# The last image of a vision layer: terms of seven states scaled token-major by ScalarE and transposed into PSUM by TensorE, the image before it finished in 24 half steps

## The chip, the cores and the metric

The kernel runs on one core of a Trainium2 chip. The metric is the device time of one execution in microseconds. A core has five engines with instruction queues of their own that work in program order: TensorE (PE; its weight loads are shown as PEld), VectorE (DVE), ScalarE (ACT), GpSimd (POOL) and SyncE (SP), which here only issues transfers. They meet in semaphores: an instruction raises one when it is done, another engine's queue waits for its value.

## The reference

Four images of 1024 tokens with 64 features pass one layer. It has a retention part, a selective scan and a routed feed-forward part, with a layer norm behind each of the last two:

```python
# retention
q, k, v = x @ Wq + bq, x @ Wk + bk, x @ Wv + bv
h = prelu(((gamma * (q @ k.T)) @ v) @ Wo + bo)
# selective scan, 128 channels, 16 states each
x_main, x_gate = split(h @ W_in + b_in)
xc = silu(x_main @ W_conv + b_conv)
B, C = split(xc @ W_bc + b_bc)                  # 16 numbers of each per token
dt = softplus(xc @ W_dt + b_dt)
for t in range(1024):
    s = exp(dt[t][:, None] * A) * s + dt[t][:, None] * B[t][None, :] * xc[t][:, None]
    y[t] = (s * C[t][None, :]).sum(-1)
h = layernorm(h + (y * silu(x_gate)) @ W_out + b_out)
# feed-forward: 64 groups of 64 tokens, each with its own expert
f = relu(h @ Wi.T + bi)
for l in range(2): f = relu(f @ shared[l] + f @ expert[l, route] + biases + f)
h = layernorm(h + f @ Wo.T + bo)
```

## The kernel before

The 128 channels of the scan lie on the partitions, the tokens along the free dimension. For each state a *job* computes `h[t] = decay[t] * h[t-1] + u[t] * B[t]` with one scan instruction of VectorE (L1336), where `decay = exp(delta * neg_a[state])` and `u = delta * xc`. Then `hc = h * C` is made ("weighed") by GpSimd (`weigh`, L1207), and TensorE adds hc, transposed, to the bank `acc_y` (`states_out`, L663). B and C are rows in DRAM (`bc_dram`), which SyncE loads broadcast over all partitions into `b_row` and `c_row` (three buffers each).

A job of the first three images has 1024 tokens. In the last image (`SPLIT`, `ALONE`) there are 32 jobs of 512 tokens: 16 states of the first half of the tokens, then the same 16 of the second. The last h of a job of the first half is kept in `carry` and starts the job of the same state in the second; ScalarE copies it (`save_carry`, L957).

The term u*B is made in one of two ways. For a job of `VECTOR_JOBS` ScalarE copies u into a PSUM bank (`fill_slot`, L947; the name `slot` is shown as `decay` in the trace), VectorE multiplies it there by b_row (`drive`, L1308), and ScalarE puts the decay into `decay_own` (`own_decay`, L920). For the others GpSimd multiplies u by b_row into `ub` (`drive`, L1196) and ScalarE puts the decay into the slot (L920). The slot has two banks, taken in turn by the jobs, so a bank can be filled for job t when the scan of job t-2 is done.

The order of work is written out by hand. All engines run the same loop, `for p in PHASES: for n in range(STEPS)`; phase p scans image p, while the head of image p+1 and the tail of image p-1 go on beside it. In the last phase each step n has two half steps, 2n and 2n+1, one for each job. In a half step s of that phase ScalarE fills the slot for job s+2, does its part of the third image's tail (`last_part`) and of the first half of the last image's own tail (`half_tail(0)`), and then makes `decay_own` for job s+3. VectorE scans job s, then its parts of the tails. GpSimd weighs job s-2, then drives job s+2. TensorE issues a matmul that keeps its clock up (`keep_warm`), `states_out` of job s-4, then its parts of both tails.

The third image's tail is a chain of 19 parts m over TensorE, ScalarE and VectorE that share the one bank `tail`: y transposed (m=2), the output product (3, 4), the norm (4 to 6), the feed-forward input (6, 7), two expert layers (8 to 13), output (13, 14), norm (15, 16), rows (17, 18). Part m is done in half step `2 + 8 * m // 5` (L295). The tables `HALF_PE`, `HALF_ACT` and `HALF_DVE` give the half steps 20 to 31 to the parts of `half_tail(0)`: y at 20, norm 22 and 23, expert layers from 25 and 27, second norm 29 and 30. After the last scan `end_of_program` does the same for the second half of the tokens.

Before the last phase, in phase 2, the head of the last image makes its bc (n=10), delta (n=12) and u (n=13).

Of the kernel before, what the change touches and what calls it, by code (L numbers as in the profile page):

```python
# [23 lines left out]
P = 128  # L24
# [22 lines left out]
for _b in range(IMAGES):  # L47
    for _first in (0, HALF) if _b in SPLIT else (0,):
        for _s in range(STATES):
# [6 lines left out]
VECTOR_JOBS = [q for q, job in enumerate(JOBS)  # L56
               if job.state in ((0, 4, 8, 10, 14) if job.image not in SPLIT else range(0, STATES, 2))]
GPSIMD_JOBS = [q for q in range(len(JOBS)) if q not in VECTOR_JOBS]
# [37 lines left out]
LAST_STEPS = 19  # L96
RELUS = (USE_L1, USE_L1 + 1, USE_L2, USE_L2 + 1)
# [33 lines left out]
def vit_layer(nc, xT, gammaT, packed, routed_w, route, out):  # L131
    with ExitStack() as ctx:
# [56 lines left out]

        late_w = gam[:, 4:8, :].rearrange("p a (g l h) -> p (a g) l h", l=LAYERS, h=HID)  # L190
# [43 lines left out]
        carry_saved = sem("carry_saved")  # L234
        hc_own = sem("last_hc_by_vector_ready")
# [53 lines left out]
        def last_steps(p, n, i):  # L289
# [44 lines left out]
        def gpsimd_made(q):  # L334

            return JOBS[q].at - vector_made(q)
# [9 lines left out]
        def ub_made(q):  # L346

            return (ub_own, vector_made(q) + JOBS[q].halves) if on_vector(q) else (ub_ready, gpsimd_made(q) + JOBS[q].halves)

# [64 lines left out]
        def _(sp):  # L414
# [26 lines left out]
            def load_b(k):  # L441
# [79 lines left out]
        def _(pe):  # L521
# [145 lines left out]

            def begin_tail(b, use):
# [159 lines left out]
            for p in range(-1, IMAGES):  # L828
                for n in range(STEPS):
# [7 lines left out]
                    for i, (start, end) in enumerate(parts(p, n)):  # L837
# [65 lines left out]
        def _(act):  # L903
# [20 lines left out]
            def own_decay(q):  # L924

                made, halves = vector_made(q), JOBS[q].halves
                if made >= 2:

                    act.wait_ge(scan_done, end_of(job_with(vector_made, VECTOR_JOBS, made + halves - 3)))
# [22 lines left out]
            def save_carry(q):  # L952

                job = JOBS[q]
                act.wait_ge(scan_done, end_of(q))
                at = ring(job.at, 1).stop - 1
                nc.scalar.activation(carry[:, job.state:job.state + 1], h[:, at:at + 1], ACT.Copy).then_inc(carry_saved, 1)  # L957
# [69 lines left out]
            def last_part(b, n):  # L1027
# [4 lines left out]
                if b == ALONE - 1 and DVE_TAIL.get(n) in RELUS:  # L1032
# [528 lines left out]
```

## Time and profile before

| what | value |
|---|---|
| median of 3 runs | 344.54 us (343.37 to 346.07) |
| the profiled execution | 343.26 us |
| its span in the profile | 340.9 us |
| mean granted TensorE clock | 0.915 |
| busy share PE, DVE, ACT, POOL | 83, 77, 56, 76 % |

The span runs from the first to the last instruction of the profiled execution. A busy share is a mean over stages with different limits, so the stage of the last image has to be read by itself.

### The profile page before, as it was taken

The page shows a single profiled execution, that of the slowest core. Times are in us where ns is not written, and L with a number is a line of the kernel's source. Part 1 is how long each engine was busy: PE and PEld are TensorE (multiplying, and loading weights), DVE is VectorE, ACT ScalarE, POOL GpSimd, SP SyncE. Part 2 cuts the span into 40 slices and gives each one's busy share as a digit, 9 for nine tenths or more (in the row PEclk, how much of TensorE's full clock was granted, in tenths as well). Part 3 has the DMA queues.
Part 4 walks back from the last instruction along what each step waited for, and adds up shares of the span by engine and source line. Part 5 has one row for each costly group of instructions (what it writes and reads, how often), then busy time and mean ns, then how long its engine had stood idle before and what let it go on. Part 6 is the DMA issues. An engine that isn't in the chain of part 4 may idle for free.

```text
span 340.9 us, 4748 instructions
## 1 busy us (share of the span) xinstructions
PE 284.1 (83%) x1462; PEld 164.4 (48%) x1462; DVE 262.5 (77%) x287; ACT 190.5 (56%) x298; POOL 259.4 (76%) x136
## 2 busy tenths in 40 slices
PE   8898839875677789989896799996975989977896
PEld 5423412333336233355662344565854668755664
DVE  2565678998778999998899799988979899575420
ACT  3004831336896342589855516799277768655422
POOL 1028057999899999998998969989999999993200
PEclk9999957999589799999799799996598999978999
DMA  7970496676779997866799967668999999980200
GB/s 236 409 294 0 147 317 218 211 280 215 249 278 308 343 358 260 285 256 232 306 279 329 344 217 273 216 244 287 296 326 330 329 376 362 301 278 25 48 0 15
DMA packets 47128, 85.88 MB, mean 252 GB/s; under 512 B 7936, under 2 KB 24832, under 8 KB 46848
## 3 DMA queue, kind: packets, MB, share of 16 engines
q1 hardware_dynamic: 46704, 84.43, 73.7%
q10 hardware_dynamic: 400, 1.17, 1.1%
q8 instruction: 11, 0.18, 0.2%
q14 instruction: 13, 0.11, 0.1%
HBM read 75.62 MB, written 1.57 MB: 226 GB/s over the span
## 4 chain that ended last, share of the span: by engine, by line
PE 28%; DVE 15%; ACT 12%; issue 4%; POOL 2%; DVEq 0%; ACTq 0%; POOLq 0%
DVE h L1336 10%; PE acc_y L663 5%; PE tail L722 4%; ACT decay L920 2%; PE acc_r L616 2%; PE work L605 2%; DVE decay L1308 2%; POOL ub L1196 2%; PE tail L677 1%; PE tail L707 1%; PE work L539 1%; PE decay L539 1%; ACT decay_own L920 1%; PE work L754 1%; PE tail L698 1%
## 5 line engine op out<-in xcount | busy, mean ns | idle before, releaser
L1207 POOL TENSOR_TENSOR hc<-h,c_row 128x1024 f32<-128x1024 f32 (+1 forms) x79 | 154.6, 1966 | 24.3 <-DVE h L1336 20.9
L1196 POOL TENSOR_TENSOR ub<-u,b_row 128x1024 f32<-128x1024 f32 (+1 forms) x49 | 98.3, 2006 | 11.5 <-DVE u L1382 11.1
L920 ACT ACTIVATE decay<-delta,neg_a 128x512 f32<-128x512 f32 (+1 forms) x64 | 51.4, 813 | 64.0 <-DVE h L1336 63.5
L663 PEld LDWEIGHTS acc_y<-pack,hc 128*128 128x128 f32 x512 | 62.7, 150 | 43.0 <-issue 23.3
L663 PE MATMUL acc_y<-pack,hc 128*128 128x128 f32 x512 | 76.0, 291 | 6.7 <-ACT y_t L1030 3.6
L1336 DVE TENSOR_TENSOR_SCAN h<-decay,ub 128x512 f32<-128x512 f32 (+1 forms) x41 | 65.9, 1608 | 11.5 <-ACT decay L920 5.7
L605 PE MATMUL work<-q,kT 64*128 64x512 f32 x112 | 36.4, 729 | 16.3 <-DVE mixed L1362 11.9
L1362 DVE TENSOR_TENSOR mixed<-gam,work 128x512 f32<-128x512 f32 x56 | 35.6, 676 | 8.2 <-PE work L605 7.5
L947 ACT ACTIVATE decay<-u 128x512 f32<-128x512 f32 (+1 forms) x42 | 26.4, 639 | 21.8 <-DVE h L1336 21.5
L616 PE MATMUL acc_r<-mixed,v_sb 128*64 128x512 f32 x128 | 36.4, 648 | 1.1 <-DVE mixed L1362 1.0
L1336 DVE TENSOR_TENSOR_SCAN h<-decay_own,decay 128x512 f32<-128x512 f32 (+1 forms) x23 | 34.5, 1499 | 1.1
L1308 DVE TENSOR_TENSOR decay<-decay,b_row 128x512 f32<-128x512 f32 (+1 forms) x40 | 30.6, 764 | 6.0 <-ACT decay L947 4.3
L920 ACT ACTIVATE decay_own<-delta,neg_a 128x512 f32<-128x512 f32 (+1 forms) x31 | 28.5, 919 | 1.4 <-DVE delta L1375 1.4
L722 PEld LDWEIGHTS tail<-f,group_w 128*128 128x128 f32 x192 | 26.3, 213 | 0.4
L722 PE MATMUL tail<-f,group_w 128*128 128x64 f32 x192 | 25.6, 293 | 0.0
L605 PEld LDWEIGHTS work<-q,kT 64*128 64x128 f32 x112 | 9.5, 207 | 32.9 <-DVE mixed L1362 22.5
L1336 DVE TENSOR_TENSOR_SCAN h<-decay,h,ub 128x512 f32<-128x512 f32 x18 | 23.1, 1283 | 2.5
L1181 POOL TENSOR_TENSOR expert_w<-expert_w 128x2048 f32<-128x2048 f32 x2 | 9.0, 4541 | 15.2 <-DMA expert_w<-routed_w 15.2
L616 PEld LDWEIGHTS acc_r<-mixed,v_sb 128*64 128x64 f32 x128 | 6.7, 143 | 28.0 <-issue 19.7
L1336 DVE TENSOR_TENSOR_SCAN h<-decay_own,h,decay 128x512 f32<-128x512 f32 x9 | 11.5, 1280 | 0.3
L539 PE MATMUL work<-gam 128*128 128x256 f32 x36 | 11.7, 413 | 0.0
L986 ACT ACTIVATE hT<-acc_r,pack 128x512 f32<-128x512 f32 x4 | 2.7, 674 | 15.8 <-PE acc_r L616 15.8
(208 smaller groups left out, 356.6 us busy)
## 6 DMA issues: line engine op xcount, KB each, us to landing
b_row<-bc_dram SPq DMA_DIRECT2D x64, 512.0 KB, 5.4
c_row<-bc_dram SPq DMA_DIRECT2D x64, 512.0 KB, 5.5
group_w<-expert_w SPq DMA_DIRECT2D x48, 128.0 KB, 4.7
gam<-gammaT SPq DMA_DIRECT2D x8, 512.0 KB, 10.6
expert_w<-routed_w SPq DMA_DIRECT2D x1, 2048.0 KB, 18.3
gam<-expert_w SPq DMA_DIRECT2D x16, 128.0 KB, 5.3
x_in<-xT SPq DMA_DIRECT2D x4, 256.0 KB, 8.6
pack<-packed ACTq DMA_DIRECT2D x1, 788.0 KB, 6.6
```

What stands on the lines that cost most here:

```text
L539: nc.tensor.matmul(bank[:, 0:2 * INNER], gam[:, 0, 0:P], gam[:, 0, 0:2 * INNER], start=True, stop=True)
L605: nc.tensor.matmul(pair[:, i * HALF:(i + 1) * HALF], kT[D * i:D * i + D, j * P:(j + 1) * P], q2[D * i:D * i + D, :], start=True, stop=True ...
L616: mm = nc.tensor.matmul(acc_r[D * i:D * i + D, :], v_sb[:, j, :], mixed[:, j % 2, i * HALF:(i + 1) * HALF], start=(j == 0), stop=(j == TIL ...
L663: mm = nc.tensor.matmul(acc_y[:, to:to + P], hc[:, at:at + P], ident, start=(job.state == 0 and c % 4 == 0), stop=(job.state == STATES - 1 ...
L722: mm = nc.tensor.matmul(bank[:, (g % 8) * GROUP:(g % 8 + 1) * GROUP], group_w[:, g, layer, :], f[:, g * GROUP:(g + 1) * GROUP], start=Fals ...
L920: op = nc.scalar.activation(target, delta[:, job.image % 2, columns], ACT.Exp, scale=neg_a[:, job.state:job.state + 1])
L947: nc.scalar.activation(slot[:, two_banks(at, halves)], u[:, job.image % 2, columns], ACT.Copy)\
L1196: nc.gpsimd.tensor_tensor(ub[:, ring(made, job.halves)], u[:, job.image % 2, tokens(q)], b_row[:, ring(job.at, job.halves)], ALU.mult).the ...
L1207: nc.gpsimd.tensor_tensor(hc[:, here], h[:, here], c_row[:, here], ALU.mult).then_inc(hc_ready, job.halves)
L1308: nc.vector.tensor_tensor(slot[:, here], slot[:, here], b_row[:, columns], ALU.mult).then_inc(ub_own, halves)
L1336: nc.vector.tensor_tensor_scan(h[:, ring(at, halves)], factor, term, initial, ALU.mult, ALU.add)\
L1362: nc.vector.tensor_tensor(mixed[:, j % 2, at], gam[:, j, at], pair[:, at], ALU.mult).then_inc(read, 1)
```

## The change

`PLACED_STATES` gives seven even states (2 to 14) of the last image, in both halves of its tokens, a third way. TensorE transposes u of the whole image (`transpose_u`, eight transposes) and bc (`transpose_bc`, two); ScalarE reads both out to SBUF (`read_u_t`, `read_bc_t`). With tokens on the partitions B[t] is one number per partition: ScalarE multiplies four 128x128 tiles of the transposed u by it (`scale_terms`), and TensorE transposes them into the job's slot bank (`place_terms`), where the scan reads them. Of the last image's 32 jobs 14 are placed, 6 are VectorE's own (states 0, 5, 11; 16 jobs before), and 12 are GpSimd's (16 before). Where only one of a pair of states still needs its row, half of b_row is loaded. ScalarE's `save_carry` becomes a copy by VectorE behind its scan. The four relus of the third image's expert layers go from ScalarE to VectorE. The third image's tail gets a table of half steps, `TAIL_AT`, that ends at 23 in place of 30. In half steps 24 to 31 TensorE issues a `keep_warm` matmul each, as it did only in 2 to 19.

```diff
+PLACED_STATES = {IMAGES - 1: (2, 4, 6, 8, 10, 12, 14)}
+PLACED_JOBS = [q for q, job in enumerate(JOBS) if job.state in PLACED_STATES.get(job.image, ())]
+VECTOR_JOBS = [q for q, job in enumerate(JOBS) if job.state in ((0, 4, 8, 10, 14) if job.image not in SPLIT else (0, 5, 11))]
+KEPT_JOBS = sorted(VECTOR_JOBS + PLACED_JOBS)
+GPSIMD_JOBS = [q for q in range(len(JOBS)) if q not in KEPT_JOBS]
...
+TAIL_AT = (2, 3, 4, 5, 6, 7, 9, 10, 12, 13, 14, 15, 17, 18, 19, 20, 21, 22, 23)
...
+        u_t = {0: y_t, ALONE: kT}
+        bc_t = {0: ln_x, ALONE: x_in}
+        placed_rows = {0: (f[:, :], f[:, :]), ALONE: (q2[:, :], v_sb[:, :, :].rearrange("p c d -> p (c d)"))}
...
-                steps += [(p - 1, m) for m in range(LAST_STEPS) if 2 + 8 * m // 5 == 2 * n + i]
+                steps += [(p - 1, m) for m in range(LAST_STEPS) if TAIL_AT[m] == 2 * n + i]
...
-                        sp.wait_ge(*ub_made(q))
-                sp.dma_start(into(b_row, k), rows(k, 0)).then_inc(b_loaded[k % 3], 16)
+                        if q not in PLACED_JOBS:
+                            sp.wait_ge(*ub_made(q))
+                wanted = [q for q in begun(2 * k, 2 * k + 2) if q not in PLACED_JOBS]
+                if b in SPLIT and len(wanted) == 1:
+                    job = JOBS[wanted[0]]
+                    sp.dma_start(b_row[:, ring(job.at, 1)],
+                                 bc_dram[b, job.state, tokens(wanted[0])].partition_broadcast(P)).then_inc(b_loaded[k % 3], 16)
+                elif wanted:
+                    sp.dma_start(into(b_row, k), rows(k, 0)).then_inc(b_loaded[k % 3], 16)
...
+            def transpose_u(b):
+
+                pe.wait_ge(u_ready, b + 1)
+                if b == ALONE:
+                    pe.wait_ge(work_read, FIRST_WORK_USES + WORK_USES * ALONE)
+                for i in range(2):
...
+                    for c in range(TILES // 2):
+                        at = i * HALF + c * P
+                        mm = nc.tensor.transpose(target[:, c * P:(c + 1) * P], u[:, b % 2, at:at + P], ident)
+                    mm.then_inc(u_t_full, 1)
+
+            def place_terms(q):
+
+                job = JOBS[q]
+                pe.wait_ge(term_ready, placed_made(q) + job.halves)
+                pe.wait_ge(scan_done, job.at + job.halves - 2)
+                rows_sb = placed_rows[job.image][placed_made(q) % 2]
+                for c in range(job.halves * TILES // 2):
+                    at = two_banks(job.at, job.halves).start + c * P
+                    mm = nc.tensor.transpose(slot[:, at:at + P], rows_sb[:, c * P:(c + 1) * P], ident)
+                mm.then_inc(term_placed, job.halves)
...
                         if p == ALONE and WARM_FROM <= 2 * n + i < WARM_TO:
 
+                            if 2 * n + i == WARM_FROM:
+                                pe.wait_ge(u_t_read, 2 * order_of_placed(ALONE) + 2)
                             keep_warm(work[:, HALF:T], 1)
+                        if p == ALONE and 2 * n + i >= 24:
+                            if 2 * n + i == 24:
+                                pe.wait_ge(tail_read, TAIL_SETUP + TAIL_USES * ALONE)
+                            keep_warm(tail, 1)
+                        for q in begun(start + 1, end + 1) if p == ALONE else begun(start + 2, end + 2):
+                            if q in PLACED_JOBS and (p == ALONE or JOBS[q].image == 0):
+                                place_terms(q)
                         for q in ended(start - 4, end - 4):
                             states_out(q)
...
+                    if head == ALONE and n == 11:
+                        transpose_bc(ALONE)
+                    if head == ALONE and n == 14:
+                        transpose_u(ALONE)
...
-            def save_carry(q):
...
+            def scale_terms(q):
...
+                if placed_left(q):
+                    act.wait_ge(term_placed, placed_left(q))
+                rows_sb = placed_rows[job.image][made % 2]
+                for c in range(job.halves * TILES // 2):
+                    token = job.first // P + c
+                    at = token % 2 * P + 2 * STATES * (token // 2) + job.state
+                    op = nc.scalar.activation(rows_sb[:, c * P:(c + 1) * P], u_t[job.image][:, token * P:(token + 1) * P],
+                                              ACT.Identity, scale=bc_t[job.image][:, at:at + 1])
+                op.then_inc(term_ready, job.halves)
...
-                if b == ALONE - 1 and DVE_TAIL.get(n) in RELUS:
-                    use = DVE_TAIL[n]
...
+                    if head == ALONE and n == 15:
+                        read_u_t(ALONE)
                     for i, (start, end) in enumerate(parts(p, n)):
                         for q in begun(start + 2, end + 2):
-                            fill_slot(q)
+                            if q not in PLACED_JOBS:
+                                fill_slot(q)
...
-                            if own_limit(start) <= JOBS[q].at < own_limit(end) and on_vector(q):
+                            if own_limit(start) <= JOBS[q].at < own_limit(end) and q in KEPT_JOBS:
                                 own_decay(q)
+                                if q in PLACED_JOBS:
+                                    scale_terms(q)
+                    if head == ALONE and n == 12:
+                        read_bc_t(ALONE)
...
+                if job.halves == 1 and job.first == 0:
+
+                    dve.wait_ge(scan_done, end_of(q))
+                    last = ring(job.at, 1).stop - 1
+                    nc.vector.tensor_copy(carry[:, job.state:job.state + 1], h[:, last:last + 1]).then_inc(carry_saved, 1)
...
-                if use in RELUS and b < ALONE - 1:
+                if use in RELUS:
```

## Rows read from the trace of the kernel before

**Rows 1.** The page, part 1: busy us (share of span) xinstructions.
```profile
PE 284.1 (83%) x1462; PEld 164.4 (48%) x1462; DVE 262.5 (77%) x287; ACT 190.5 (56%) x298; POOL 259.4 (76%) x136
```

**Rows 2.** Busy us by stretch: PE, PEld, DVE, ACT, POOL, clock, DMA share, GB/s.
```profile
251.00:280.00 29.00, 22.05 (x121) 16.19 (x119) 26.48 (x29) 22.49 (x50) 28.11 (x23) 0.94 1.05 342
280.00:320.60 40.60, 33.76 (x221) 26.50 (x221) 27.16 (x30) 24.75 (x49) 31.12 (x26) 0.92 0.69 222
302.50:309.00 6.50, 6.42 (x26) 5.62 (x27) 2.12 (x2) 2.02 (x4) 5.23 (x5) 0.53 0.63 208
```

**Rows 3.** GpSimd in order of time: start us, us, line, out<-in [idle before <-releaser].
```profile
258.52 2.50 POOL L1207 TENSOR_TENSOR hc<-h,c_row 128x512 f32<-128x512 f32 x2 [0.16 <-DMA c_row<-bc_dram]
...
262.63 2.50 POOL L1207 TENSOR_TENSOR hc<-h,c_row 128x512 f32<-128x512 f32 x2
265.10 1.26 POOL L1196 TENSOR_TENSOR ub<-u,b_row 128x512 f32<-128x512 f32 x1
...
313.68 2.49 POOL L1207 TENSOR_TENSOR hc<-h,c_row 128x512 f32<-128x512 f32 x2 [5.95 <-DVE h L1336]
```

**Rows 4.** VectorE in order of time, an earlier stage and the last one.
```profile
213.94 1.22 DVE L1336 TENSOR_TENSOR_SCAN h<-decay,ub 128x512 f32<-128x512 f32 x1
215.30 1.28 DVE L1336 TENSOR_TENSOR_SCAN h<-decay,h,ub 128x512 f32<-128x512 f32 x1
...
251.08 0.70 DVE L1308 TENSOR_TENSOR decay<-decay,b_row 128x512 f32<-128x512 f32 x1 [1.27 <-ACT decay L947]
...
255.70 1.22 DVE L1336 TENSOR_TENSOR_SCAN h<-decay_own,decay 128x512 f32<-128x512 f32 x1
256.84 1.20 DVE L1336 TENSOR_TENSOR_SCAN h<-decay,ub 128x512 f32<-128x512 f32 x1
...
279.95 0.67 DVE L1308 TENSOR_TENSOR decay<-decay,b_row 128x512 f32<-128x512 f32 x1
...
297.91 0.42 DVE L1426 TENSOR_TENSOR gam<-gam,work 128x256 f32<-128x256 f32 x1 [2.51 <-ACT work L1095]
...
310.68 0.69 DVE L1406 TENSOR_TENSOR ln_y<-ln_x,tail 128x512 f32<-128x512 f32 x1 [5.92 <-ACT tail L1049]
...
319.33 1.27 DVE L1336 TENSOR_TENSOR_SCAN h<-decay,carry,ub 128x512 f32<-128x512 f32 x1
```

**Rows 5.** VectorE in order of time, two small operations of the setup.
```profile
34.41 0.14 DVE L1301 COPY b_c<-tail 128x2 f32<-128x2 f32 x1
34.48 0.27 DVE L1286 CAST bias_w<-pack 96x256 bf16<-96x256 f32 x1
```

**Rows 6.** ScalarE in order of time: ahead of the stage, and in it.
```profile
248.68 0.69 ACT L1041 ACTIVATE ln_q<-tail,b_c 128x512 f32<-128x512 f32 x1 [0.68 <-PE tail L698]
...
260.52 0.59 ACT L947 ACTIVATE decay<-u 128x512 f32<-128x512 f32 x1
261.04 0.19 ACT L957 ACTIVATE carry<-h 128x1 f32<-128x1 f32 x1
261.13 0.68 ACT L920 ACTIVATE decay<-delta,neg_a 128x512 f32<-128x512 f32 x1
261.75 0.19 ACT L957 ACTIVATE carry<-h 128x1 f32<-128x1 f32 x1
...
295.28 0.47 ACT L1082 ACTIVATE gam<-acc_r,b_c 128x256 f32<-128x256 f32 x1
295.64 0.47 ACT L1086 ACTIVATE gam<-acc_r,b_c 128x256 f32<-128x256 f32 x1
```

**Rows 7.** TensorE in order of time, the last stage.
```profile
260.15 0.63 PE L663 MATMUL acc_y<-pack,hc 128*128 128x128 f32 x4 [3.58 <-ACT y_t L1030]
...
267.59 1.08 PE L698 MATMUL tail<-f,w_out_c 128*64 128x512 f32 x4
...
279.14 1.89 PE L722 MATMUL tail<-f,group_w 128*128 128x64 f32 x16
...
281.36 0.60 PE L663 MATMUL acc_y<-pack,hc 128*128 128x128 f32 x4
281.80 0.60 PE L539 MATMUL work<-gam 128*128 128x256 f32 x2
```

More of the change, by code:

```diff
@@ L348, in ub_made, with b_loads @@
             return (ub_own, vector_made(q) + JOBS[q].halves) if on_vector(q) else (ub_ready, gpsimd_made(q) + JOBS[q].halves)
+        def b_loads(k):
+            return 16 * sum(s % 3 == k % 3 and any(q not in PLACED_JOBS for q in begun(2 * s, 2 * s + 2)) for s in range(k + 1))
         def ring(at, halves):
@@ L950, in fill_slot, with read_bc_t, read_u_t @@
                         decay_exp(q, slot[:, two_banks(at, halves)], columns)
-            def save_carry(q):
[L954 to L957, printed above, removed]
+            def read_bc_t(b):
+                act.wait_ge(bc_t_full, order_of_placed(b) + 1)
+                if b == 0:
+                    act.wait_ge(s_bias, BIAS_STEPS)
+                source = acc_r if b == ALONE else tail
+                nc.scalar.activation(bc_t[b][:, 0:2 * P], source[:, 0:2 * P], ACT.Copy).then_inc(bc_t_read, 1)
+            def read_u_t(b):
+                before = 2 * order_of_placed(b)
+                for i in range(2):
+                    columns = slice(i * HALF, (i + 1) * HALF)
+                    act.wait_ge(u_t_full, before + i + 1)
+                    source = work[:, columns] if b == ALONE else tail[:, :]
+                    nc.scalar.activation(u_t[b][:, columns], source, ACT.Copy).then_inc(u_t_read, 1)
+            def scale_terms(q):
+                job, made = JOBS[q], placed_made(q)
+                if job.image == ALONE and made == placed_made(PLACED_JOBS[0]) or q == PLACED_JOBS[0] or \
+                        JOBS[PLACED_JOBS[PLACED_JOBS.index(q) - 1]].image != job.image:
+                    act.wait_ge(u_t_read, 2 * order_of_placed(job.image) + 2)
+                    act.wait_ge(bc_t_read, order_of_placed(job.image) + 1)
+                if placed_left(q):
[7 more added lines that the diff above has]
+                op.then_inc(term_ready, job.halves)
             def first_evictions():
@@ L1138, in _ @@
                             side_eviction(head, SIDE_AT[n])
-                        for q in ended(start, end):
-                            if JOBS[q].halves == 1 and JOBS[q].first == 0:
-                                save_carry(q)
                         for b, m in last_steps(p, n, i):
@@ L1216, in _ @@
                         for q in begun(start + 2, end + 2):
-                            if not on_vector(q):
+                            if q in GPSIMD_JOBS:
                                 drive(q)
@@ L1316, in scan_job @@
                     here = two_banks(at, halves)
-                    if on_vector(q):
-                        drive(q, here, ring(at, halves), vector_made(q) + done)
-                        factor, term = decay_own[:, two_banks(vector_made(q) + at - job.at, halves)], slot[:, here]
+                    if q in KEPT_JOBS:
+                        if on_vector(q):
+                            drive(q, here, ring(at, halves), vector_made(q) + done)
+                        else:
+                            dve.wait_ge(term_placed, placed_made(q) + job.halves)
+                        factor, term = decay_own[:, two_banks(kept_made(q) + at - job.at, halves)], slot[:, here]
                     else:
@@ L1325, in scan_job @@
                         dve.wait_ge(hc_ready, at + halves - 6)
-                        old = JOBS[JOB_OF[at + halves - 7]]
-                        if old.halves == 1 and old.first == 0:
-                            dve.wait_ge(carry_saved, old.state + 1)
                     initial = 0.0
```

52 lines of the change are left out of this document (39 added, 13 removed).

## The prediction, made before the changed kernel ran

> **What bounds the kernel now.** I read first the page's busy shares [rows 1]: TensorE, VectorE and GpSimd are all at 76 to 83 per cent, so the whole-span average names nobody, and the question is what ends last in the stage that the diff touches. That is the last image's scan stage: its 32 half steps (one job of 512 tokens each, which I call step 0 to step 31) run from VectorE's first multiply at 251.08 us to the end of the last scan at 320.60 us, 69.5 us. Behind it lies a fixed end of 20.3 us (the second half's feed-forward part), which the diff leaves as it is.
>
> The busy times by stretch [rows 2] and GpSimd's order of time [rows 3] show the first 56 us of it: GpSimd is busy 28.11 of 29.00 us in steps 0 to 15. Two weighings take 2.47 us and a drive 1.27, so two steps cost it 3.7 us. VectorE (26.48 of 29.00) keeps pace just behind. In steps 16 to 31 the picture is another: 40.6 us, of which VectorE works 27.2. Its order of time [rows 4] shows where the rest went: a wait of 2.51 us at 297.91 and one of 5.92 us at 310.68, both for ScalarE's logarithm step of a layer norm. The second is the third image's last norm, which stands behind the last image's own layers on TensorE. GpSimd then idles too, 5.95 us [rows 3]. So there are two things to win: GpSimd's load, and that collision.
>
> **The change, part by part.** Times are summed against the profiled execution (343.26 us: 340.9 of span and 2.4 around it). The median of the runs is 1.28 us above it, and I carry that over.
>
> *GpSimd.* 16 drives in the stage become 12. Four fewer at about 1.24 us of spacing is 5.0 us, which leaves 44 operations, 54.6 us. The b_row loads of 14 of the 16 pairs halve; GpSimd hardly waits for them now [rows 3], so this gives nothing by itself.
>
> *VectorE.* 16 multiplies become 6. Each costs 0.70 us between its start and the scan behind it (251.08 and 279.95 are such multiplies; the duration is 0.67 to 0.70): ten are 7.0 us, five of them in each half. Four relus of 512 columns come over from ScalarE; a multiply of that width lasts 0.67 to 0.70, and without a wait behind it I put one at 0.6: 2.4 us, half in each half. The 16 carry copies come over too, each with a wait for VectorE's own scan, all in steps 0 to 15. A scan with no such wait is followed after 1.14 us (255.70 to 256.84), one whose successor waits for it after 1.36 us (213.94 to 215.30) [rows 4]; a 128x2 copy keeps the engine 0.07 us (34.41 to 34.48) [rows 5]. So a carry costs at most 0.22+0.07 = 0.29 and at least 0.07; I take 0.26, nearest to the row with the wait, 4.2 us in all. Steps 0 to 15: 26.5 - 3.5 + 1.2 + 4.2 = 28.4 us of VectorE work, more than the 26.5 before. Steps 16 to 31: 27.2 - 3.5 + 1.2 = 24.9.
>
> A rule of the Trainium skill bears on this term: VectorE: DVE Perf Modes, section "The DRAIN you can't avoid", says that a semaphore behind each operation costs nothing extra, since the flush is paid anyway. By it 16 carries would cost only their copies, 1.1 us and not 4.2, and the forecast would be 3 us lower; the rows above speak against it, since they show 0.22 us for the wait.
>
> *ScalarE.* It gives up ten copies of u (0.52 us apart: 5.2), 16 carries (0.09: 1.5) and four relus (2.1), 8.8 us. It takes on 14 jobs of four 128x128 scalings. None is in the trace. Below them lies the 128x1 copy at 0.09, above them the 128x256 operation with a pointer at 0.36 [rows 6]; the 128x512 exponential from SBUF at 0.62 less 384 columns at 0.43 us per 512 gives 0.29, which I take: 1.16 us a job and 16.2 us in all (5 to 20). Net +7.4 us, and what matters more: they stand in the middle of ScalarE's queue. In an odd step it evicts the next slot, then does its part of the third image's tail, and only then decay and scalings of the job three steps on.
>
> *TensorE.* A placement is four transposes, like one states_out: 0.44 us of spacing (281.36 to 281.80), 0.60 to its end [rows 7]. 14 are 6.1 us. They stand in its queue in odd steps, behind the matmuls of the step before. Before, TensorE's lateness in this stage hit only states_out, which nobody waited for soon; now a scan waits for it. A product of 512 fp32 columns lasts about 1.1 us (267.59), a layer's 16 expert matmuls 1.9 (279.14).
>
> *Ahead of the stage.* Eight transposes of u now stand in front of the second image's output product. ScalarE's square at 248.68 waited for that product [rows 6], and from it a chain runs over two operations, decay_own and the u copy into VectorE's first multiply, which waited 1.27 us for it [rows 4]. That is 2 x 0.44 = 0.9 us. Then the two reads of u, 2 x 0.52 = 1.0, stand in front of the same copy. Start: +1.9 us. The transposes and the read of bc fall where ScalarE has slack: 0.
>
> **The walk.** With those prices I follow the four queues, one step at a time (clock at its upper level). In steps 0 to 15 VectorE waits: at step 4 for TensorE's y transposes, because ScalarE, busy with scalings, copies y 1.2 us later; at step 8 for the placement behind residual, keep-warm, states_out and output product (0.9); at step 10, since scalings stand behind square, centred copy, logarithm and exponential (1.5); at step 12 for a placement (0.7) and then for layer 1's matmuls (1.7). That is 6.0 us of waits, against 2.5 now: 28.4 + 6.0 = 34.4 us, 5.4 more than 29.0. In steps 16 to 31 it waits at 18 for layer 2 (1.1), at 20 behind the output residual (0.9), at 21 for the last norm and the half tail's y (2.8), at 23 for the half tail's norm (1.6), at 28 and 30 for placements behind the half tail's two layers (1.4 and 2.5), at 31 (0.5). That is 10.8: 24.9 + 10.8 = 35.7 us, 4.9 less than 40.6: the collision is gone, most of its gain eaten by placements queued behind layers.
>
> The clock: TensorE stood still 3.58 us ahead of 260.15 [rows 7]. From 302.5 to 309.0 its granted clock was 0.53, mostly the lower level (1.2 GHz) [rows 2]. The walk has a gap of 2.3 us in step 20, where TensorE waits for y behind ScalarE's scalings and norm. Should the clock fall, about six transposes and small products on the path take twice 0.4 us: +2.4 us, and some 1 us at step 4. I take 1.5 (0 to 4). The new keep-warm matmuls from step 24 work in the other direction and are in the walk.
>
> Sum: +1.9 + 5.4 - 4.9 + 1.5 = +3.9 us. So 344.5 + 3.9 = 348.4 us, the last scan's start at about 322 to 323 us in place of 319.33.
>
> **Rivals.**
> - *GpSimd's relief arrives (faster).* If ScalarE and TensorE keep ahead of VectorE, the stage is bounded by GpSimd's 54.6 us and the remaining waits for the half tail (some 5). Less 5.0 for the drives and less 5.9 for the collision, plus 1.9 at the start: -9.0, 335.5 us. It decides where a placement ends before VectorE comes free in at least ten of the 14 jobs. For it speaks that ScalarE and TensorE have gaps now (22.5 and 22.1 of 29.0 busy in the first half [rows 2]); against it, that both do their work in fixed order behind tail waits. In its weaker form half of the walk's waits go: 340 us. Chance 0.24.
> - *The two sides cancel.* The waits of steps 0 to 15 are 2 to 4 us shorter than walked (scalings at 0.2, carries at 0.1) and the clock holds: 344.5 us (341 to 348). Chance 0.31.
> - *The forecast*, queues of ScalarE and TensorE on the scan's path: 348.4 (345 to 352), most of it over 1 per cent slower. Together with the next, 0.45 for slower.
> - *The clock falls in both halves.* With placements on the path, a late TensorE delays VectorE, which delays TensorE. With a level of 0.5 through half of the stage, 14 placements and the two layers cost 8 us more than the upper level: about 353. The chance of that within the 0.45 is 0.10.
> - *Transfers.* That smaller b_row loads make GpSimd faster: its waits for them are under 0.4 us each [rows 3], so under 1 us.
>
> **How the numbers follow.** About 1 per cent (3.4 us) is what a measurement can tell from no change: under 341.1 is faster (0.24), 341.1 to 348.0 the same (0.31), above it slower (0.45). 8 in 10 leaves out the strong form of the first rival and the far end of the clock's: 338 to 354. The likeliest case alone spans 345 to 352.
>
> **What would show it.** Right: VectorE's waits for the transposed terms (TensorE into the slot) total 4 to 8 us; the first multiply of step 16 starts at 285 to 289 us instead of 279.95; GpSimd idles over 10 us before the last scan; the carry copy adds 0.2 us or more; the scalings are 0.29 us apart; the wait for ln_y falls from 5.9 to 2 to 3 us. Wrong: GpSimd still back to back through step 15 with its drives ahead, or scans in placed steps following at 1.2 us.

## The result and the profile after

| | before | changed |
|---|---|---|
| median | 343.96 us (342.61 to 346.07, 4 runs) | 352.71 us (349.35 to 355.41, 4 runs) |
| ratio | | 1.0222, 95 % interval 1.0163 to 1.0281 |
| the profiled execution | 343.26 us, span 340.9 | 354.54 us, span 352.8 |

The change makes the kernel 2.2 per cent slower, 8.7 us by the medians against the 3.9 forecast. A ratio leaves out, on both sides, executions over 1.5 per cent above the fastest of the same kernel. The profiled execution is one of the slower of its four; I come back to why. Between the two profiled executions the last scan moved by 11.7 us (319.33 to 331.00).

The page of the changed kernel, part 1, answers to [rows 1]. GpSimd and VectorE work less, TensorE and ScalarE more:

```profile
PE 299.3 (85%) x1544; PEld 175.3 (50%) x1544; DVE 261.6 (74%) x297; ACT 199.1 (56%) x327; POOL 254.6 (72%) x132
```

The busy times by stretch answer to [rows 2]. The columns are the same: busy us of PE, PEld, DVE, ACT, POOL, then the granted clock. The first two lines are steps 0 to 15 and 16 to 31, the next two parts of the first, the last the end behind the scans:

```profile
253.40:295.90 42.50, 35.00 (x178) 26.16 (x178) 27.23 (x41) 27.21 (x59) 26.18 (x22) 0.80 0.66 206
295.90:332.30 36.40, 33.00 (x231) 26.03 (x232) 25.06 (x27) 27.14 (x67) 26.45 (x22) 1.00 0.57 169
256.90:262.20 5.30, 5.21 (x25) 4.94 (x26) 3.55 (x6) 3.92 (x10) 3.50 (x3) 0.59 0.94 274
278.10:288.50 10.40, 10.40 (x29) 6.07 (x28) 4.49 (x7) 5.63 (x14) 4.81 (x4) 0.51 0.88 270
332.30:352.80 20.50, 17.10 (x102) 12.24 (x102) 3.62 (x8) 5.59 (x14) 0.00 (x0) 1.00 0.06 14
```

Steps 0 to 15 took 29.0 us and take 42.5; steps 16 to 31 took 40.6 and take 36.4. GpSimd, which had bound the first stretch with 28.1 of 29.0 us, is busy 26.2 of 42.5. In the first stretch the clock's mean is 0.80, with two parts near the lower level; in the second it is the upper one throughout. The end behind the scans takes 20.5 us, as before (20.3).

VectorE in order of time, start and duration, shows what it waits for (in the brackets); it answers to [rows 4]:

```profile
253.38 0.70 DVE L1428 TENSOR_TENSOR decay<-decay,b_row 128x512 f32<-128x512 f32 x1 [3.09 <-ACT decay L1043]
254.11 1.22 DVE L1456 TENSOR_TENSOR_SCAN h<-decay_own,decay 128x512 f32<-128x512 f32 x1
255.37 0.15 DVE L1462 COPY carry<-h 128x1 f32<-128x1 f32 x1
255.45 0.69 DVE L1531 TENSOR_TENSOR ln_y<-ln_x,tail 128x512 f32<-128x512 f32 x1
...
262.38 1.22 DVE L1456 TENSOR_TENSOR_SCAN h<-decay_own,decay 128x512 f32<-128x512 f32 x1 [1.47 <-PE decay L748]
...
277.84 1.22 DVE L1456 TENSOR_TENSOR_SCAN h<-decay_own,decay 128x512 f32<-128x512 f32 x1 [1.82 <-PE decay L748]
...
286.15 1.22 DVE L1456 TENSOR_TENSOR_SCAN h<-decay_own,decay 128x512 f32<-128x512 f32 x1 [4.83 <-PE decay L748]
...
290.68 0.69 DVE L1522 TENSOR_SCALAR f<-tail 128x512 f32<-128x512 f32 x1 [3.13 <-PE tail L805]
...
295.93 0.69 DVE L1428 TENSOR_TENSOR decay<-decay,b_row 128x512 f32<-128x512 f32 x1
...
310.88 0.69 DVE L1531 TENSOR_TENSOR ln_y<-ln_x,tail 128x512 f32<-128x512 f32 x1 [2.50 <-ACT tail L1170]
...
328.91 1.28 DVE L1456 TENSOR_TENSOR_SCAN h<-decay_own,carry,decay 128x512 f32<-128x512 f32 x1 [2.46 <-PE decay L748]
...
331.00 1.28 DVE L1456 TENSOR_TENSOR_SCAN h<-decay,carry,ub 128x512 f32<-128x512 f32 x1
```

The wait for ln_y did fall from 5.92 to 2.50 us. In its place stand waits for L748, the placement. The view of who waited for whom, here from 253.4 to 332.3 us, sums them (total us, times, longest):

```profile
POOL hc L1327 <- DVE h L1456: 24.4, 14, 3.9
DVE h L1456 <- PE decay L748: 14.9, 9, 4.8
```

Nine of the 14 placements came late, by 14.9 us together. And TensorE's order of time around the worst one, step 12 at 286.15 [rows 7 for the same operations at the upper level]:

```profile
277.15 0.66 PE L748 MATMUL decay<-pack,q 128*128 128x128 f32 x4 [1.85 <-ACT q L1078]
277.64 0.60 PE L704 MATMUL acc_y<-pack,hc 128*128 128x128 f32 x4
278.17 1.93 PE L790 MATMUL tail<-h1T,pack 64*128 64x512 f32 x2
280.03 1.22 PE L580 MATMUL work<-gam 128*128 128x256 f32 x2
281.04 1.06 PE L704 MATMUL acc_y<-pack,hc 128*128 128x128 f32 x4
282.03 2.07 PE L790 MATMUL tail<-h1T,pack 64*128 64x512 f32 x2
284.04 1.22 PE L580 MATMUL work<-gam 128*128 128x256 f32 x2
285.05 1.06 PE L748 MATMUL decay<-pack,v_sb 128*128 128x128 f32 x4
```

TensorE stood still 1.85 us for ScalarE's scalings of job 10. From 278.17 to 288.5 everything lasts about twice as long: states_out takes 1.06 us and not 0.60. The terms of job 12 were scaled by 282.6 (four scalings, 1.26 us together, from 281.33; ScalarE had read the first input product of the third image's feed-forward part before them). Their placement at 285.05 then stands behind the second input product (282.03) and keep-warm matmuls.

### The profile page after: what moved, and what is told of

It reads as the page before. It is cut to its first block, busy times and chain, and to the rows that moved or that the text cites. A ratio compares the mean times of both kernels' runs of the same rounds, so it can differ in the third digit from the quotient of the medians.

```text
span 352.8 us, 4928 instructions
## 1 busy us (share of the span) xinstructions
PE 299.3 (85%) x1544; PEld 175.3 (50%) x1544; DVE 261.6 (74%) x297; ACT 199.1 (56%) x327; POOL 254.6 (72%) x132
## 4 chain that ended last, share of the span: by engine, by line
PE 34%; DVE 12%; ACT 10%; issue 3%; POOL 2%; DVEq 0%; ACTq 0%; POOLq 0%
DVE h L1456 8%; PE acc_y L704 7%; PE tail L805 4%; PE work L580 2%; PE decay L748 2%; PE acc_r L657 2%; PE work L646 2%; PE tail L790 2%; POOL ub L1316 2%; ACT decay L1016 2%; ACT decay_own L1016 1%; PE tail L760 1%; PE tail L781 1%; PE tail L580 1%; PE decay L580 1%
## 5 line engine op out<-in xcount | busy, mean ns | idle before, releaser
L1327 POOL TENSOR_TENSOR hc<-h,c_row 128x1024 f32<-128x1024 f32 (+1 forms) x79 | 154.8, 1964 | 42.7 <-DVE h L1456 37.8
L1316 POOL TENSOR_TENSOR ub<-u,b_row 128x1024 f32<-128x1024 f32 (+1 forms) x45 | 93.1, 2069 | 10.8 <-DVE u L1507 10.8
L1016 ACT ACTIVATE decay<-delta,neg_a 128x512 f32<-128x512 f32 (+1 forms) x60 | 48.6, 820 | 70.3 <-DVE h L1456 70.1
L704 PE MATMUL acc_y<-pack,hc 128*128 128x128 f32 x512 | 77.7, 294 | 2.9 <-POOL hc L1327 2.8
L1456 DVE TENSOR_TENSOR_SCAN h<-decay,ub 128x512 f32<-128x512 f32 (+1 forms) x39 | 63.6, 1631 | 11.4 <-ACT decay L1016 5.8
L646 PE MATMUL work<-q,kT 64*128 64x512 f32 x112 | 37.3, 746 | 15.6 <-DVE mixed L1487 11.2
L1456 DVE TENSOR_TENSOR_SCAN h<-decay_own,decay 128x512 f32<-128x512 f32 (+1 forms) x25 | 36.9, 1476 | 10.9 <-PE decay L748 9.9
L657 PE MATMUL acc_r<-mixed,v_sb 128*64 128x512 f32 x128 | 36.4, 648 | 1.1 <-DVE mixed L1487 1.0
L1016 ACT ACTIVATE decay_own<-delta,neg_a 128x512 f32<-128x512 f32 (+1 forms) x35 | 31.3, 895 | 1.9 <-DVE delta L1500 1.4
L1428 DVE TENSOR_TENSOR decay<-decay,b_row 128x512 f32<-128x512 f32 (+1 forms) x30 | 23.8, 793 | 7.3 <-ACT decay L1043 6.1
L1043 ACT ACTIVATE decay<-u 128x512 f32<-128x512 f32 (+1 forms) x32 | 20.4, 652 | 15.4 <-DVE h L1456 15.2
L657 PEld LDWEIGHTS acc_r<-mixed,v_sb 128*64 128x64 f32 x128 | 6.7, 143 | 28.1 <-issue 19.7
L1456 DVE TENSOR_TENSOR_SCAN h<-decay_own,carry,decay 128x512 f32<-128x512 f32 x10 | 12.8, 1276 | 5.0 <-PE decay L748 4.9
L1522 DVE TENSOR_SCALAR f<-tail 128x512 f32<-128x512 f32 x12 | 8.2, 683 | 5.0 <-PE tail L805 4.7
## 6 DMA issues: line engine op xcount, KB each, us to landing
gam<-gammaT SPq DMA_DIRECT2D x8, 512.0 KB, 10.8
```

What stands on the lines that cost most here:

```text
L646: nc.tensor.matmul(pair[:, i * HALF:(i + 1) * HALF], kT[D * i:D * i + D, j * P:(j + 1) * P], q2[D * i:D * i + D, :], start=True, stop=True ...
L657: mm = nc.tensor.matmul(acc_r[D * i:D * i + D, :], v_sb[:, j, :], mixed[:, j % 2, i * HALF:(i + 1) * HALF], start=(j == 0), stop=(j == TIL ...
L704: mm = nc.tensor.matmul(acc_y[:, to:to + P], hc[:, at:at + P], ident, start=(job.state == 0 and c % 4 == 0), stop=(job.state == STATES - 1 ...
L1016: op = nc.scalar.activation(target, delta[:, job.image % 2, columns], ACT.Exp, scale=neg_a[:, job.state:job.state + 1])
L1043: nc.scalar.activation(slot[:, two_banks(at, halves)], u[:, job.image % 2, columns], ACT.Copy)\
L1316: nc.gpsimd.tensor_tensor(ub[:, ring(made, job.halves)], u[:, job.image % 2, tokens(q)], b_row[:, ring(job.at, job.halves)], ALU.mult).the ...
```

## The experiments

Each run's ratio is to the runs of the kernel before on the same chip, with a 95 per cent interval. "Last scan" is where it starts in the profiled execution: 319.33 us before, 331.00 in the changed kernel.

| run | what differs from the changed kernel | ratio | last scan |
|---|---|---|---|
| changed | | 1.022 (1.016 to 1.028) | 331.00 |
| e1 | only tail table and late keep-warm, on the kernel before | 0.997 (0.993 to 1.001) | |
| e2 | more keep-warm, steps 0 to 19 | 1.024 (1.014 to 1.033) | 330.16 |
| e3 | old tail spacing | 1.005 (1.001 to 1.009) | 323.92 |
| e4 | carries and relus on ScalarE | 1.033 (1.025 to 1.042) | 330.37 |
| e5 | ScalarE's decays and scalings ahead of tail parts | 1.046 (1.038 to 1.055) | 333.32 |
| e6 | more keep-warm, steps 0 to 11 | 1.022 (1.017 to 1.027) | 326.62 |
| e7 | transposed u made and read later | 1.035 (1.028 to 1.041) | 330.64 |
| e8 | only states 5 and 11 placed, transposed u as in e7, else as before | 1.018 (1.013 to 1.023) | 325.17 |
| e9 | e3 and e6 together | 1.024 (1.013 to 1.034) | 324.73 |
| e10 | e3, e7, more keep-warm in steps 0 to 3 | 1.011 (1.003 to 1.019) | 321.43 |
| e11 | e10 with relus on ScalarE | 1.016 (1.007 to 1.024) | 320.64 |

**The pace of the tail, alone and with placements (e1, e3).** e1 puts two parts of the change on the kernel before (the table `TAIL_AT` comes with them):

```diff
-                steps += [(p - 1, m) for m in range(LAST_STEPS) if 2 + 8 * m // 5 == 2 * n + i]
+                steps += [(p - 1, m) for m in range(LAST_STEPS) if TAIL_AT[m] == 2 * n + i]
...
+                        if p == ALONE and 2 * n + i >= 24:
+                            if 2 * n + i == 24:
+                                pe.wait_ge(tail_read, TAIL_SETUP + TAIL_USES * ALONE)
+                            keep_warm(tail, 1)
```

> The kernel before with two parts of the change alone: the third image's tail by the new table of half steps (ends at 23, not 30) and the keep-warm matmuls of half steps 24 to 31. No placed states, carries and relus stay on ScalarE. Theory 'the collision can be won without placements': the 5.9 us wait of VectorE for ln_y falls under 2.5 us and the time is 3 to 6 us under before (338 to 341). Rival 'the faster tail itself makes the queues wait': parts that are closer together stall TensorE and ScalarE in the first 16 half steps as well, time within 2 us of before or above it.

Measured: 343.69 us against 345.67, ratio 0.997 (0.993 to 1.001). The collision could not be won that way; the rival's "within 2 us of before" holds. Its profiled execution was the slowest of its eleven (349.65 us), so no time of the stage is taken from it; but VectorE's wait for ln_y, at 303.37, is still 4.94 us there, where the first theory wanted under 2.5.

e3 takes the same parts out of the changed kernel:

```diff
-                steps += [(p - 1, m) for m in range(LAST_STEPS) if TAIL_AT[m] == 2 * n + i]
+                steps += [(p - 1, m) for m in range(LAST_STEPS) if 2 + 8 * m // 5 == 2 * n + i]
...
-                        if p == ALONE and 2 * n + i >= 24:
-                            if 2 * n + i == 24:
-                                pe.wait_ge(tail_read, TAIL_SETUP + TAIL_USES * ALONE)
-                            keep_warm(tail, 1)
```

> The changed kernel with the old spacing of the third image's tail (parts at 2+8m//5, to half step 30) and without the keep-warm matmuls of half steps 24 to 31. Theory 'placements on the scan's path are what costs': still over 350, the collision of ln_y with the last image's layers comes back and makes it 352 to 357. Rival 'the faster tail is what costs': 344 to 348.

Measured: 346.96 us, ratio 1.005. My own theory had asked for over 350 and falls; the rival's 344 to 348 holds. So with the slow tail the rest of the change, placements and all, costs half a per cent, on the kernel before the fast tail costs nothing, and both together cost 2.2. Two of e3's ten executions took 353.74 and 353.92 us, with a mean clock of 0.913 and 0.908. So the slow tail does not rule out executions with a low clock; there were two of ten with it and two of four of the changed kernel. Who waited for whom in e3 shows the late placements halved:

```profile
DVE h L1452 <- PE decay L748: 7.1, 8, 1.8
```

and its stretches show the upper level in 277 to 287, where the changed kernel ran at the lower:

```profile
257.00:262.00 5.00, 5.00 (x25) 4.72 (x24) 3.18 (x6) 3.96 (x9) 3.57 (x3) 0.59 0.95 249
277.00:287.00 10.00, 7.48 (x41) 4.95 (x41) 5.62 (x9) 6.91 (x15) 7.95 (x7) 1.00 0.94 319
```

**Is it the clock? (e2, e6, e9).** e2 adds keep-warm matmuls:

```diff
-WARM_FROM, WARM_TO = 2, 20
+WARM_FROM, WARM_TO = 0, 20
...
-                            keep_warm(work[:, HALF:T], 1)
+                            keep_warm(work[:, HALF:T], 3 if 2 * n + i < 2 else 2)
```

> The changed kernel with more keep-warm matmuls in the last image's stage: three in half steps 0 and 1 (none there now), two instead of one in 2 to 19. Theory 'the clock': the two stretches at the lower level (0.59 and 0.51 of full clock, 15.7 us together) cost 5 to 8 us; with the clock up they vanish and the time is 345 to 348 against some 352. Theory 'queues alone': each added matmul of 0.43 us stands ahead of a placement, the time is 1 to 4 us longer than the changed kernel's (353 to 356).

Measured: 354.06 us, no gain, as the queue theory had it. The trace shows that both were half right. The clock stayed up to step 20, and scan 16 started at 292.00 against 296.66; then steps 16 to 31 took 38.2 us from first scan to last, not 34.3, with 0.66 of the clock in 307 to 312:

```profile
307.00:312.00 5.00, 3.40 (x18) 2.67 (x16) 2.52 (x4) 4.50 (x12) 1.70 (x2) 0.66 0.95 232
```

e6 keeps the added matmuls to the first 12 steps (three in steps 0 and 1, two in 2 to 11, one from 12):

> The changed kernel with the added keep-warm matmuls of the first clock run (three in half steps 0 and 1, two in 2 to 11) but one as before from 12 on. In the first clock run the upper level held to 307 us, the first scan of half step 16 came 4.7 us earlier than in the changed kernel, and half steps 16 to 31 took 3.8 us longer. If that loss was the added matmuls in 12 to 19, the time is now 347 to 350; if the clock brings nothing that stays, 352 to 355.

Measured: 350.50 us, just outside the 347 to 350 of the clock theory. Its stage runs at the upper level from end to end; two of the stretches:

```profile
257.00:262.00 5.00, 4.84 (x36) 4.51 (x36) 4.25 (x7) 4.19 (x10) 3.99 (x4) 1.00 1.00 265
277.00:287.00 10.00, 10.00 (x61) 7.61 (x61) 5.43 (x9) 6.41 (x15) 5.62 (x5) 1.00 0.80 251
```

Execution against execution its last scan is 4.4 us earlier (326.62 and 331.00), net of what the added matmuls cost. By the ratios nothing is gained (1.022 both), by the medians 2.2 us. The changed kernel's own executions say why these differ: the two with a mean clock of 0.903 and 0.908 took 354.5 and 355.4 us, the two with 0.936 and 0.926 took 349.4 and 350.9. So some executions probably lose the clock for less time, and 4 to 6 us go with it (their traces were not kept); e6, with 349.8 to 351.2, sits where the two quick ones are.

e9 has e6's keep-warm in steps 0 to 19 and the old tail, so that the clock is up in both, and the pace and the late keep-warm matmuls differ:

> Old tail spacing, as in the run that kept the rest of the change, with the keep-warm matmuls of the second clock run (three in half steps 0 and 1, two in 2 to 11, one to 19). Against that second clock run (350.5 us, the upper level throughout, tail to 23) the pace of the tail is all that differs, the clock is up in both. Theory 'the compressed tail costs by queueing, whatever the clock': 344 to 346, 5 us or more under 350.5. Theory 'the compressed tail costs mainly by letting the clock fall': within 2 us of 350.5.

Measured: 348.96 us, ratio 1.024, within 2 us of e6, as the theory has it that the fast tail costs mainly by letting the clock fall. The last scans agree, 324.73 and 326.62: with the clock up the pace costs 1.9 us; with it free to fall, 7.1 (e3 and changed). The scan of step 16 shows where. It starts at 291.89 in e9 and 292.29 in e6, 0.4 us apart; in e3 it starts at 291.08 and in the changed kernel at 296.66, 5.6 apart. From there to the last scan the fast tail takes 1.5 us longer in both pairs (34.3 and 32.8 us), and the late keep-warm matmuls can have their part only in these 1.5 us.

The comparison of e9 with e3 shows the price of the remedy: where the clock in 277 to 287 was up anyway, the added matmuls took nothing off. In the profiled executions e9 is 0.8 us behind e3, by the medians 2.0 (348.96 and 346.96), by the ratios 1.8 per cent, since the kernel before ran 2.5 us slower beside e3 (345.67 and 343.13). How much slower e9 is than e3 is thus known only to lie between 0.8 us and some 6.

**VectorE's added work (e4, e11).** e4 gives the carry copies and relus back to ScalarE:

```diff
-                    dve.wait_ge(scan_done, end_of(q))
-                    last = ring(job.at, 1).stop - 1
-                    nc.vector.tensor_copy(carry[:, job.state:job.state + 1], h[:, last:last + 1]).then_inc(carry_saved, 1)
...
+                        for q in ended(start, end):
+                            if JOBS[q].halves == 1 and JOBS[q].first == 0:
+                                save_carry(q)
```

> The changed kernel with the 16 carry copies and the four relus given back to ScalarE. Theory 'VectorE's added work costs' (my term of 4.2 us for carries and 2.4 for relus): 3 to 6 us faster than the changed kernel. Theory 'VectorE waits for placements anyway': its own work is hidden in its waits, and ScalarE gets 16 x 0.1 + 4 x 0.5 = 3.6 us more in front of scalings: from 1 us faster to 3 us slower than the changed kernel.

Measured: 355.54 us against the changed kernel's 352.71. But all four executions of e4 have a mean clock of 0.903 to 0.908, and the two of the changed kernel with such a clock took 354.5 and 355.4 us; the last scan is 0.6 us earlier in e4's trace. So it is within the rival's range, not clearly slower. VectorE waits longer for what it saved, 18.5 us for placements and once 5.0 for the decay of job 12, which ScalarE's queue held up:

```profile
DVE h L1476 <- PE decay L748: 18.5, 9, 3.3
DVE h L1476 <- ACT decay_own L1016: 5.0, 1, 5.0
```

So taking off VectorE the 4.2 and 1.2 us of steps 0 to 15, terms of my sum, gave no gain. As the same work went into ScalarE's queue, e4 does not show what VectorE's share alone is worth. e11 tries the relus alone, on e10:

> As the run before it, with the four relus of the third image back on ScalarE. VectorE waited 4.2 us for the layer matmuls in the old-tail run with its relus on it. If those waits are VectorE's alone, 2 to 4 us are won against the run before it; if ScalarE's scalings now wait in their place, as with the carries, 0 to 3 us are lost.

Measured: 346.77 against 345.52, the intervals overlap. In its trace the last scan is even 0.8 us earlier. Nothing won or lost that can be told.

**ScalarE's order (e5).**

```diff
+                        if p == ALONE:
+                            for q in range(len(JOBS)):
+                                if own_limit(start) <= JOBS[q].at < own_limit(end) and q in KEPT_JOBS:
+                                    own_decay(q)
+                                    if q in PLACED_JOBS:
+                                        scale_terms(q)
                         for b, m in last_steps(p, n, i):
                             last_part(b, m)
                         if p == ALONE and 2 * n + i in HALF_ACT:
                             half_tail(0, HALF_ACT[2 * n + i])
...
```

> The changed kernel with ScalarE's decay and scalings of a half step put ahead of its parts of the two tails, so that a placement no longer waits behind a norm or the y copy. Theory 'ScalarE's queue order is what makes placements late': VectorE's waits for placements, 14.9 us in the changed kernel, fall under 9 us and the time by 3 to 5 us (347 to 349). Rival 'TensorE's order is what makes them late': waits stay over 12 us, and the tail parts come later by 1 to 2 us each, time within 2 us of the changed kernel's or above it.

Measured: 359.84 us, the slowest of all. The waits for placements fell by only 2.5 us, to 12.4, and the tail parts came late by more than I had thought, because they in turn hold up TensorE and VectorE:

```profile
DVE h L1463 <- PE decay L748: 12.4, 10, 3.7
DVE gam L1558 <- ACT work L1211: 5.7, 2, 5.2
DVE ln_y L1538 <- ACT tail L1170: 3.7, 1, 3.7
DVE f L1524 <- PE tail L776: 3.5, 1, 3.5
```

In these two orders there is no slack between the two duties: whichever ScalarE does first, VectorE waits for the other. How much of the loss is the order itself stays open, since the granted clock fell in four stretches here, among them 307 to 317 us (mean 0.66), where the changed kernel kept the upper level.

**The start (e7, e10).** Both engines make and read the transposed u behind what the next scans need:

```diff
-                    if head == ALONE and n == 14:
-                        transpose_u(ALONE)
...
                         for b, m in last_steps(p, n, 0):
                             last_part(b, m, LATE)
+                    if head == ALONE and n == 14:
+                        transpose_u(ALONE)
```

> The changed kernel with the eight transposes of u behind the second image's output product on TensorE, and ScalarE's two reads of them behind the slot fills of half steps 0 and 1, directly before the first scalings. My step 'start +1.9 us' says: the first multiply comes 2 to 3 us earlier (250.5 to 251.5 in place of 253.38), and the time is 1.5 to 2.5 us shorter than the changed kernel's if that lead stays. Rival: the next scans wait for the later scalings instead, and the lead is gone by half step 4, same time as the changed kernel's.

Measured: 354.18 us. The first scan starts at 252.29, 1.8 us earlier; at step 4 the lead is 0.4 us (262.02 and 262.38), and 0.4 at the last scan. The rival holds, though by the ratio, 1.035, e7 is slower than the changed kernel: all its four executions have a mean clock of 0.903 to 0.909, and their 354.07 to 356.82 us go with the changed kernel's 354.5 and 355.4. e10 adds old tail and, in steps 0 to 3, keep-warm matmuls:

> Old tail spacing, transposes and reads of u moved behind the first slot fills, three keep-warm matmuls in half steps 0 and 1, two in 2 and 3, one to 19; the rest as changed. If the lower level in half steps 0 to 4 is what took the earlier start back, the start (2 us) and the placement of half step 4 (1.5 us) are won: 342 to 344.5, at or under before. If the start is lost again, 346 to 348.

Measured: 345.52 us against 343.13, ratio 1.011 (1.003 to 1.019), above the 342 to 344.5 hoped for. The upper level holds through the stage, the first scan starts at 250.77, 1.0 us before that of the kernel before, scan 4 at 259.66 against 262.13 in e3, so the lead did stay. Yet scan 16 starts at 288.60 where before has 280.66. These are its longer waits from step 10 to 15:

```profile
271.92 1.22 DVE L1452 TENSOR_TENSOR_SCAN h<-decay_own,decay 128x512 f32<-128x512 f32 x1 [0.61 <-PE decay L748]
276.25 0.69 DVE L1527 TENSOR_TENSOR h1T<-ln_x,tail 128x512 f32<-128x512 f32 x1 [0.84 <-ACT tail L1166]
...
281.42 1.22 DVE L1452 TENSOR_TENSOR_SCAN h<-decay_own,decay 128x512 f32<-128x512 f32 x1 [1.47 <-PE decay L748]
285.93 0.69 DVE L1518 TENSOR_SCALAR f<-tail 128x512 f32<-128x512 f32 x1 [3.10 <-PE tail L805]
```

With the old table the first relu, now VectorE's, stands at step 14, and VectorE waits 3.10 us there for the first expert layer; before, ScalarE did this relu and waited 1.11 us for the layer. In the second half e10 wins 5.8 us (scan 16 to 31: 32.8 against 38.7), in the first it loses 9.0 (scan 0 to 16: 37.8 against 28.9).

**A light version (e8).** Only states 5 and 11, GpSimd's before, are placed; carries, relus and tail as before:

```diff
-PLACED_STATES = {IMAGES - 1: (2, 4, 6, 8, 10, 12, 14)}
+PLACED_STATES = {IMAGES - 1: (5, 11)}
...
-VECTOR_JOBS = [q for q, job in enumerate(JOBS) if job.state in ((0, 4, 8, 10, 14) if job.image not in SPLIT else (0, 5, 11))]
+VECTOR_JOBS = [q for q, job in enumerate(JOBS) if job.state in ((0, 4, 8, 10, 14) if job.image not in SPLIT else range(0, STATES, 2))]
...
```

> The kernel before with only two states placed, 5 and 11, in both halves: four jobs taken from GpSimd, VectorE's 16 multiplies, ScalarE's carries and relus and the old tail spacing as before, with the start of the run above. Theory 'GpSimd bounds half steps 0 to 15 of before': four drives less give up to 2.5 us in each half, 339 to 342. Rival 'the queues' slack was GpSimd's only in name': what bounds next (VectorE's own 28 us, the wait for ln_y) takes it back, 343 to 347.

Measured: 348.98 us, over the rival's range too. Each of the four placements came late, by 1.04, 1.82, 2.51 and 3.96 us:

```profile
DVE h L1472 <- PE decay L748: 9.3, 4, 4.0
```

So the loss does not go with the number of placed jobs: four cost 1.8 per cent here, 14, with the rest of the change, cost 0.5 in e3. The longest wait fits the queues: the scalings (308.65) stand behind parts of two norms on ScalarE, the placement (311.55) behind layer matmuls on TensorE at the lower level. GpSimd's relief of 5 us brought no gain. None of the eleven runs beats the kernel before by more than its interval.

## Why the prediction was right, and where it was not

The direction, the mechanism and most terms held. Two terms were sized too low, the clock and the queueing in steps 0 to 15, and with them the total. The median, 352.71, lies above the likeliest case's 345 to 352 and next to the 353 of a rival that had a chance of 0.10; two of the four executions lie above 354. Of the signs named, GpSimd's idleness (24.4 us), the wait for ln_y, the scalings' spacing and the carry's cost came as said. The waits for placements (14.9 us against 4 to 8), the first multiply of step 16 (295.93 against 285 to 289) and the last scan (331.00 against 322 to 323) did not.

- **GpSimd and the collision.** Twelve drives, the ln_y wait from 5.92 to 2.50 (2 to 3 forecast), GpSimd idle: as said, and off the path.
- **Start, +1.9 us.** The first multiply started at 253.38, +2.3 us. e7 shows that the term is not additive: 1.8 us won there were 0.4 by step 4, in a stretch at the lower level. e10 kept the lead where the clock stayed up.
- **Scalings, 0.29 us apart.** The trace bears it out: ScalarE's next operation starts 1.16 us after the first of four (308.42 and 309.58), and four at 0.29 are 1.16.
- **Carry, 0.26 us.** A copy starts 1.26 us after its scan, not 1.14, and the next operation 0.08 to 0.11 later: 0.20 to 0.23 us, 3.2 to 3.7 in all in place of 4.2. The Trainium skill's statement weighed there (VectorE: DVE Perf Modes, "The DRAIN you can't avoid") is that a semaphore behind each operation costs nothing extra. It does not cover an operation that waits for that semaphore, and in this trace the wait costs 0.12 us, so the forecast was right not to go by it. e4 gave the copies and relus back and won nothing.
- **Steps 16 to 31.** Forecast 35.7 us with 10.8 of waits; measured 36.4. The waits stand where the walk put them and nowhere else: 0.34 and 1.11 at step 18, 0.90 at 20, 2.50 and 0.16 at 21, 2.07 at 23, 1.21 at 28, 2.46 at 30, 0.47 at 31, together 11.2.
- **Steps 0 to 15.** Forecast 34.4, measured 42.5. The walk put waits at 4, 8, 10, 12 and the relu of 12, 6.0 us together; they are 1.47 and 1.30 at 4, 1.48 at 8, 1.82 at 10, 4.83 at 12, 3.13 at the relu, 14.0 us. The walk had no placement late at step 4; the other places are right, and the sizes are too low, most at step 12, where it had 0.7 and 1.7. The walk counted TensorE at the upper level. In e6, which ran there, the same waits are 0.64 and 1.30, 2.34, 1.73, 2.06 and 1.85, together 9.9 us.
- **The clock, +1.5 us (0 to 4).** This is the term that failed most. I put the fall at step 20, behind a gap of 2.3 us. The gap there was 1.60 us and the clock held. It fell behind a gap of 4.54 us at step 1 and, in the profiled execution, of 1.85 us at step 9 (shown above). The first line is the 4.54 us gap, the second the one at which the clock held:

```profile
256.99 1.12 PE L748 MATMUL decay<-pack,q 128*128 128x128 f32 x4 [4.54 <-ACT q L1078]
311.28 0.63 PE L856 MATMUL work<-pack,y_t 128*128 128x128 f32 x4 [1.60 <-ACT y_t L1194]
```

In the profiled execution this was 15.7 us near the lower level. e6 gives 4.4 us back net of its own matmuls, up to step 16 the fast tail costs 5.6 us with the clock free to fall and 0.4 with it held up, and the four executions of the changed kernel differ by 4 to 6 us with their clock. The rival "the clock falls in both halves" had the price (353) but not the place, as it fell in one half; that the median came out at its price is luck.

- **Queueing in steps 0 to 15, +5.4 us.** The clock is not all of the miss. Start and steps 0 to 15 were forecast at +7.3 us without the clock. e3, with the slow tail, has step 16's scan 10.4 us later than before (291.08 and 280.66), though its clock fell only in 254 to 261. e6, with the fast tail and the upper level throughout, has it 11.6 us later, its own added matmuls included. So the walk put this queueing 3 to 4 us too low, above all the placements at steps 8 and 12 (2.34 and 2.06 us in e6, 0.9 and 0.7 in the walk). How much of that is e3's early fall or e6's matmuls is not settled.

## What to carry to other kernels

Before work is moved from a saturated engine to engines with gaps, follow their queues in program order: a gap in an engine that waits in a fixed order is not room, and one late instruction placed on the scan's path costs what stands ahead of it. Walk it at both levels of TensorE's clock: here a new wait of 1.85 us was followed by 10.4 us at about half speed. A change of several parts is read by taking each out: here two parts, harmless or nearly so alone, make most of the loss together.

## What was not expected of the hardware

The clock did not fall where the longest gap of my walk was. TensorE stood still 1.85 us ahead of 277.15 and ran near the lower level from 278.1 to 288.5, though it was busy 10.40 of those 10.40 us; in e3 the same operations, behind gaps of 0.87 and 1.05 us, ran at the upper one. Longer gaps than 1.85 us were passed without a fall: in e10 TensorE stood still 2.77 us ahead of 252.85, and the granted clock stayed at 1.00. Before the same transposes of y it stood still 1.60 us in the changed kernel and in e2. In the changed kernel the clock held (311.28), in e2 it fell (309.02); here are the stretches of the changed kernel and of e2:

```profile
307.00:312.00 5.00, 2.61 (x15) 1.23 (x14) 2.31 (x4) 4.97 (x13) 3.59 (x3) 1.00 0.68 191
307.00:312.00 5.00, 3.40 (x18) 2.67 (x16) 2.52 (x4) 4.50 (x12) 1.70 (x2) 0.66 0.95 232
```

Two of four executions of one kernel kept a mean clock 0.02 to 0.03 higher than the others. So it can't be read from the length of one gap whether the clock falls, and a median of few runs of such a kernel can lie 4 to 6 us off by it.
